# First attention: projections of heads 0-3 in the first half of a batch, heads 4-7 at its end, and TensorE's other work in small pieces

## The chip, the cores and the metric

The kernel runs on one core of a Trainium2 chip. Its time is the device time of one execution in microseconds. Five engines work side by side, each on its own list of instructions and in its order: PE (TensorE, matrix products), DVE (VectorE), ACT (ScalarE), POOL (GpSimd) and SP, which here only issues transfers. They meet at semaphores: an instruction adds to a count, another engine waits until the count has reached a value. Transfers (DMA) are issued by SP, ACT and POOL and run on 16 shared DMA engines.

## The reference

The network has two layers, each of an attention and a feed-forward part, on x of 16 batches, 128 rows (D) and 256 positions (T). What the change touches is the first attention, for each of the 16 batches:

```python
dk = D // NH                              # NH = 8 heads of 16
q = xt @ Wq.T                             # xt: x transposed, (T, D)
qh = q.reshape(B, T, NH, dk).transpose(0, 2, 1, 3)
scores = scale * einsum('bhqd,bhkd->bhqk', qh, qh)
logits = (scores * cmask + (1.0 - cmask) * NEG) * rmask
attn = softmax(logits, axis=-1)
ctx = einsum('bhqk,bhkd->bhqd', attn, qh)
out = ctx @ Wo.T
```

Queries, keys and values are one and the same projection. The mask is 0 or 1 for each position of a batch. Behind it come a gated feed-forward part whose weights are looked up in a table of 16 values, a second attention with 16 heads, and a mixture of four experts.

## The kernel before, in words

**Stages.** The first attention runs over the 16 batches as a software pipeline, with buffers of two batches (`par` is 0 or 1). While batch i has its scores computed for the row maxima, batch i-1 has its transposed scores, exponentials and contexts, batch i-2 is normalised and multiplied by Wo, and batch i+1 is projected. Beside this, one slice of the feed-forward weights per batch is looked up: ACT fetches one-hot rows (1 MB, `load_hot`, L549), DVE compares them (`one_hot`), PE multiplies 32 small matrices (`look_up`), ACT copies the product out (`looked_up`).

**The data of a batch.** The eight heads are four pairs; a projection (`project`, L759) makes the stacked rows of one pair, 256 columns of PSUM bank PA. Half 0 of PA is pairs 0 and 1 (heads 0-3), half 1 is pairs 2 and 3. For each half ACT writes two bf16 copies, `ks` with a constant row for the maximum and `qs` (`stacks`, L516). DVE subtracts `qs` from PA to get the low parts (`lows`, L1166). SP then patches the tiles by DMA (`patch`, L310): one transfer writes the mask's row into `ks` once `ks` is there, two write the low rows into `qs` and `ks` once `low` is there. The counts `pt0` and `pt1` tell that half 0 and half 1 have landed.

**Scores.** For c = 0..3 and s = 0, 1, `scores` writes half s of PB from the qs and ks columns of one pair, and DVE takes the row maxima of it (`maxima`, L1172). Scores with c = 0, 1 wait for `pt0`, with c = 2, 3 for `pt1`. After the eight, DVE casts the maxima, PE turns them into rows (`max_rows`), and DVE adds them to `qs` (`add_max`, counted by `q2`). Only then may `scores_T` of that batch go; each fills half s of PC, from which ACT takes exponentials (`exps`, L531). `scores_T` waits for the exponential two groups back, `scores` for the maximum two groups back. `contexts` needs all eight exponentials.

**Order of the work.** Each engine's order is written by hand in its `body`, and every wait stalls all that stands behind it on that engine. PE: c = 0: scores, scores_T for both s, then project_v (the values); c = 1: the same, then look_up; c = 2: the same, outputs0 (Wo, of batch i-2), projections 0 and 1; c = 3: the same, projections 2 and 3; then contexts, max_rows, contexts. The outputs share a PSUM bank with the look-up, so outputs0 waits until `looked_up` has read it (count `w0`). SP in `load_next` loads x and a mask and then issues patch 0 and patch 1 of the next batch, in this order. POOL masks x for a later batch once all projections of one are done, and splits contexts into parts.

**Ends.** Batches 0 and 1 are projected ahead of the loop by other code, which stays as it is; the body of the last batch has no projections (`after=False`).

Of the kernel before, what the change touches and what calls it, by code (L numbers as in the profile page):

```python
# [15 lines left out]
B, D, T = 16, 128, 256  # L16
# [23 lines left out]
LPC = 512 // (2 * LG)  # L40
# [38 lines left out]
def program(nc, x, cond, condT, consts, wqT, woT, lut, idx_all, w_emb, b_emb, g_norm, w_qkv, g_q, g_k,  # L79
            w_out, w_outT, w_r, b_r, w_all, out, tok_x, tok_r, idx_low, absent_d):  # L80
    with ExitStack() as ctx:
# [420 lines left out]
        def _(act):  # L502
# [13 lines left out]
            def stacks(b, par, h):  # L516
                o = slice(h * 512, (h + 1) * 512)
                act.wait_ge(S["pq"], 2 * b + h + 1)
                if not (isinstance(b, int) and b < 2):
                    act.wait_ge(S["st"], 8 * (b - 1))  # L520
                nc.scalar.activation(ks[:, par, o], PA[:, o], ACT.Identity, bias=cst[:, C_EV:C_EV + 1]).then_inc(S["ka"], 1)
                nc.scalar.copy(qs[:, par, o], PA[:, o]).then_inc(S["qa"], 1)

# [7 lines left out]
            def exps(b, c):  # L531
                unless_first(act, S["ctx"], b)
                for s in range(2):
                    act.wait_ge(S["st"], 8 * b + 2 * c + s + 1)
                    o = slice(s * 512, (s + 1) * 512)
                    nc.scalar.activation(probs[:, c, o], PC[:, o], ACT.Exp, scale=SCALE0).then_inc(S["ex"], 1)  # L536
# [6 lines left out]
            def looked_up(c):  # L543

                act.wait_ge(S["lmm"], c + 1)
                nc.scalar.copy(w0t[:, :, bass.ds(c * LCOLS, LCOLS)], PD[:, 512:1024].rearrange("p (h c) -> p h c", h=2)
                               ).then_inc(S["w0"], 1)
# [9 lines left out]
            def body(i, par, before=True, after=True):  # L557
                exps(i - 1, 0)
                values(i - 1, 1 - par)
                exps(i - 1, 1)  # L560
                looked_up(i - 1)
                load_hot(i + 1, 1 - par)
                exps(i - 1, 2)
                if before:
                    context_out(i - 2)
                exps(i - 1, 3)
                if after:
                    stacks(i + 1, 1 - par, 0)
                    stacks(i + 1, 1 - par, 1)

            body(1, 1, before=False)
# [179 lines left out]
        def _(pe):  # L751
# [16 lines left out]
            def project_v(b, par, half):  # L768
                pe.wait_ge(S[f"xs{par}"], 16 * (half + 1))
                unless_first(pe, S["cq"], b)  # L770
                for kt in range(KT):
                    ins = mm(PD[:, kt * P:(kt + 1) * P], xs[:, par, kt * P:(kt + 1) * P], wq1[:], start=True, stop=True)
                ins.then_inc(S["v"], 1)
# [32 lines left out]
                if s == 1:  # L806
                    ins.then_inc(S["ctx"], 1)

            def look_up(c, par):
                pe.wait_ge(S["onehot"], c + 1)  # L810
                pe.wait_ge(S["q2"], min(c + 1, B) if isinstance(c, int) else c + 1)
                if isinstance(c, int) and c >= B:
                    pe.wait_ge(S["c"], LAST)
                bank = PD[:, 512:1024].rearrange("p (h c) -> p h c", h=2)
                for j in range(LPC):
                    ins = mm(bank[:, :, j * LG:(j + 1) * LG], hot[:, par, j * P:(j + 1) * P],
                             lutw[:].rearrange("p h g -> p (h g)"), start=True, stop=True)
                ins.then_inc(S["lmm"], 1)

            def max_rows(b):  # L820
                pe.wait_ge(S["mc"], 3 * b + 3)
# [9 lines left out]
            def outputs0(b):  # L831
                pe.wait_ge(S["ct"], b + 1)
                pe.wait_ge(S["w0"], LCH if isinstance(b, int) and b == LAST else b + 2)
                for qt in range(KT):
                    ins = mm(PD[:, 512 + qt * P:512 + (qt + 1) * P], cT[:, qt * P:(qt + 1) * P], wo1[:], start=True, stop=True)
                ins.then_inc(S["wo"], 1)
# [11 lines left out]
            def body(i, par, half, before=True, after=True):  # L848
                for c in range(4):
                    for s in range(2):  # L850
                        scores(i, par, c, s)
                        scores_T(i - 1, 1 - par, c, s)
                    if c == 0:
                        project_v(i - 1, 1 - par, half)
                    if c == 1:
                        look_up(i - 1, 1 - par)
                    if c == 2 and before:
                        outputs0(i - 2)
                    if c >= 2 and after:
                        project(i + 1, 1 - par, 2 * c - 4)  # L860
                        project(i + 1, 1 - par, 2 * c - 3)
                contexts(i - 1, 1 - par, 0)
                max_rows(i)
                contexts(i - 1, 1 - par, 1)
# [267 lines left out]
        def _(dve):  # L1132
# [36 lines left out]
                o = slice(h * 512, (h + 1) * 512)  # L1169
                v.tensor_tensor(low[:, o], PA[:, o], qs[:, par, o], ALU.subtract).then_inc(S["lo"], 1)  # L1170

            def maxima(b, before=False):  # L1172
                for c in range(4):
                    for s in range(2):
                        dve.wait_ge(S["sa"], 8 * b + 2 * c + s + 1)
                        if c == s == 0:
                            unless_first(dve, S["mc"], 3 * b)
                        v.tensor_reduce(nmax[:, c, s, :], PB[:, s * 512:(s + 1) * 512].rearrange("p (a k) -> p a k", k=T),  # L1178
                                        AX.X, ALU.max, negate=True).then_inc(S["max"], 1)
                        if before and 2 * c + s < 3:  # L1180
                            normalise(b - 2, 2 * c + s + 1)
                dve.wait_ge(S["max"], 8 * b + 8)
                unless_first(dve, S["mt"], b)
                cols = mcol.rearrange("p q r (s m) -> p r s q m", s=2)
                v.tensor_copy(cols[:, :, :, :, ROW_MAX], nmax[:]).then_inc(S["mc"], 1)
                dve.wait_ge(S["mc"], 3 * b + 1)
                v.tensor_tensor(cols[:, :, :, :, ROW_MAX_LOW], nmax[:], cols[:, :, :, :, ROW_MAX], ALU.subtract).then_inc(S["mc"], 1)

                v.tensor_copy(mcol[:, :, :, ROW_ABSENT::64].rearrange("p q r s -> p q (r s)"),
                              nbig[:, :, bass.ds(b, 1)].broadcast_to([P, KT, 2 * PAIRS])).then_inc(S["mc"], 1)  # L1190

            def add_max(b, par):
                dve.wait_ge(S["mt"], b + 1)
                v.tensor_tensor(qs[:, par, :], PD[:, 512:1024].bitcast(BF16), qs[:, par, :], ALU.add).then_inc(S["q2"], 1)
# [20 lines left out]
            def body(i, par, half, before=True, after=True):  # L1215
                if before:
                    normalise(i - 2, 0)
                maxima(i, before)
                if after:
                    lows(i + 1, 1 - par, 0)  # L1220
                one_hot(i, par, half)
                add_max(i, par)
                if after:
                    lows(i + 1, 1 - par, 1)

            dve.wait_ge(S["kprep"], 1)
            lows(0, 0, 0)
# [406 lines left out]
```

## Time and profile before

| | us |
|---|---|
| median of 3 runs | 780.7 (778.14 to 783.45) |
| profiled execution | 782.84 |
| its span, first to last instruction | 781.2 |
| PE busy | 605.0 (77%) |
| DVE busy | 430.9 (55%) |
| ACT busy | 322.0 (41%) |
| POOL busy | 111.8 (14%) |
| TensorE's granted clock, mean | 0.863 of 2.4 GHz |

Busy times are sums over the span, so stages of different character are mixed. The first attention lies between about 20 and 298 us. The page cuts the span into 40 slices of 19.5 us; slices 2 to 15 hold that stage. In the rows, `small` is the one tensor that holds xs, qs, ks, low and others, `arena` holds the looked-up weights and the one-hot rows, and `wst` scratch. L764 is a projection, L772 project_v, L780 scores, L792 scores_T, L804 contexts, L816 look_up, L828 max_rows, L835 outputs0; L521 and L522 are stacks, L536 exps, L546 looked_up, L550 load_hot's issue; L1178 maxima, L1170 lows, L1164 one_hot, L1194 add_max; L317 is the issue of the two low-part transfers.

### The profile page before, as it was taken

How to read it: one execution, taken by the hardware profiler on the slowest of the kernel's cores; microseconds unless marked ns; L12 is line 12 of the kernel's file. 1: busy time of each engine (PE TensorE's matmuls, PEld its weight loads, DVE VectorE, ACT ScalarE, POOL GpSimd, SP SyncE). 2: the span in 40 equal slices, each digit the busy share in tenths (PEclk: the TensorE clock that was granted, in tenths of full speed). 3: DMA queues.
4: the chain of work that ended last, by engine and by line, in shares of the span. 5: the costliest groups of instructions: out<-in, count | busy, mean ns of one | idle time of the engine just before them, and what ended most of it. 6: DMA issues, size and time to landing. Idle time of an engine off the chain costs nothing. (4 is left out here: it accounts for less than half of the span.)

```text
span 781.2 us, 15202 instructions
## 1 busy us (share of the span) xinstructions
PE 605.0 (77%) x4891; PEld 375.2 (48%) x4923; DVE 430.9 (55%) x957; ACT 322.0 (41%) x575; POOL 111.8 (14%) x145
## 2 busy tenths in 40 slices
PE   1456788867778869999956787788628999999992
PEld 1134455544455445555533454454414666666662
DVE  2455665675665664334336999999852333333331
ACT  1133454544454543233336777777502222222220
POOL 3401111111111001000000000000011333333321
PEclk9576666786666798999989999999958999999997
DMA  8863333333333320000036566555210111111110
GB/s 281 180 166 79 75 88 96 93 93 76 75 90 87 87 73 2 1 1 0 0 76 179 126 147 146 145 147 137 75 21 28 42 41 40 38 40 43 44 34 3
DMA packets 32739, 62.42 MB, mean 80 GB/s; under 512 B 7109, under 2 KB 19975, under 8 KB 30280
## 3 DMA queue, kind: packets, MB, share of 16 engines
q1 hardware_dynamic: 22112, 23.99, 10.7%
q0 software_dynamic: 6432, 18.46, 10.5%
q10 hardware_dynamic: 4168, 19.61, 9.7%
q8 instruction: 17, 0.28, 0.2%
q14 instruction: 10, 0.08, 0.0%
HBM read 58.81 MB, written 7.82 MB: 85 GB/s over the span
## 5 line engine op out<-in xcount | busy, mean ns | idle before, releaser
L1178 DVE TENSOR_REDUCE nmax<-PB 128x2 f32<-128x512 f32 x128 | 83.7, 677 | 93.8 <-PE PB L780 93.8
L536 ACT ACTIVATE probs<-PC 128x512 f32<-128x512 f32 x128 | 69.5, 595 | 132.2 <-PE PC L792 132.1
L780 PE MATMUL PB<-small 64*128 64x256 bf16 x256 | 46.6, 377 | 69.2 <-DMA small<-small 69.2
L1562 DVE TENSOR_TENSOR probs<-PC,probs 128x1024 bf16<-128x1024 f32 x19 | 23.3, 1225 | 79.9 <-ACT probs L729 65.6
L729 ACT CAST probs<-PC 128x1024 bf16<-128x1024 f32 x19 | 19.2, 1012 | 113.7 <-PE PC L1090 95.6
L764 PE MATMUL PA<-small,wq 128*128 128x256 f32 x128 | 50.6, 534 | 13.9 <-DVE identb L1142 13.9
L1082 PE MATMUL PA<-arena,probs 128*128 x227 | 54.2, 390 | 7.7 <-issue 3.9
L780 PEld LDWEIGHTS PB<-small 64*128 64x128 bf16 x256 | 12.8, 104 | 92.0 <-issue 70.6
L1101 PE MATMUL PD<-arena,probs 128*128 x456 | 53.0, 273 | 2.5 <-issue 2.5
L1082 PE MATMUL PB<-arena,probs 128*128 x210 | 48.6, 379 | 0.9
L1101 PEld LDWEIGHTS PD<-arena,probs 128*128 128x128 bf16 x456 | 44.3, 98 | 8.3 <-issue 3.2
L792 PE MATMUL PC<-small 64*128 64x256 bf16 x256 | 46.4, 376 | 0.9 <-ACT probs L536 0.8
L455 POOL DMA_DIRECT2D arena<-in_w_all x16 | 8.5, 531 | 236.9 <-DVE arena L1416 138.0
L764 PEld LDWEIGHTS PA<-small,wq 128*128 128x128 f32 x128 | 31.1, 270 | 22.8 <-issue 19.0
L661 ACT ACTIVATE probs<-PA,gb 128x1024 f32<-128x1024 f32 x32 | 35.6, 1112 | 15.7 <-PE PA L995 15.7
L1082 PEld LDWEIGHTS PA<-arena,probs 128*128 128x128 bf16 x228 | 22.8, 100 | 35.1 <-issue 15.2
L393 POOL TENSOR_TENSOR arena<-wst,wz 128x256 f32 (+1 forms) x16 | 10.0, 625 | 201.2 <-ACT wst L541 201.2
L804 PE MATMUL PD<-probs,vu 128*32 128x256 f32 x512 | 35.1, 395 | 2.4 <-ACT probs L536 1.4
L1285 DVE TENSOR_TENSOR wst<-PB,wst 128x512 f32<-128x512 f32 (+1 forms) x24 | 16.6, 691 | 36.5 <-PE PB L920 28.2
L477 POOL DMA_INDIRECT out<-probs,tokn x19 | 19.3, 1016 | 116.8 <-DVE probs L1569 116.8
L920 PE MATMUL PB<-arena 128*128 (+1 forms) x143 | 35.8, 386 | 0.1
L920 PE MATMUL PA<-arena 128*128 (+1 forms) x133 | 33.9, 386 | 1.0 <-issue 0.6
(188 smaller groups left out, 1175.5 us busy)
## 6 DMA issues: line engine op xcount, KB each, us to landing
arena<-idx_low ACTq DMA_DIRECT2D x15, 1024.0 KB
wst<-in_w_all SPq DMA_DIRECT2D x48, 256.0 KB, 2.8
arena<-in_w_all POOLq DMA_DIRECT2D x16, 384.0 KB, 6.3
arena<-in_idx_all ACTq DMA_DIRECT2D x1, 2176.0 KB, 11.4
arena<-in_cond SPq DMA_DIRECT2D x16, 128.0 KB, 3.3
small<-in_x SPq DMA_DIRECT2D x16, 128.0 KB, 2.1
small<-small SPq DMA_DIRECT2D x64, 32.0 KB
arena<-idx_low POOLq DMA_DIRECT2D x2, 1024.0 KB, 15.2
```

Source lines behind the costliest of these rows:

```text
L477: pool.indirect_dma_start(out, bass.IndirectOffsetOnAxis(ap=tokn[:, j:j + 1], axis=0), yo[:, j % 2, :], None, bounds_check=TOK - 1, oob_is ...
L536: nc.scalar.activation(probs[:, c, o], PC[:, o], ACT.Exp, scale=SCALE0).then_inc(S["ex"], 1)
L661: nc.scalar.activation(probs[:, 2 * par + c, :], PA[:], ACT.Exp, scale=DK1 ** -0.5, bias=gb[:]).then_inc(S["e3"], 1)
L764: ins = mm(PA[:, pr * T:(pr + 1) * T], wq3[:, pr].rearrange("p a b c -> p (a b c)"), xm[:, par, :], start=True, stop=True)
L780: ins = mm(PB[:, s * 512 + qt * T:s * 512 + (qt + 1) * T], qs[r, par, c * T + qt * P:c * T + (qt + 1) * P], ks[r, par, c * T:(c + 1) * T], ...
L792: ins = mm(PC[:, s * 512 + n * T:s * 512 + (n + 1) * T], ks[r, par, pr * T + kt * P:pr * T + (kt + 1) * P], qs[r, par, pr * T:(pr + 1) * T ...
L804: ins = mm(PD[pr * HS:(pr + 1) * HS, s * T:(s + 1) * T], vu[:, par, kt, 2 * pr + s, :], probs[:, (pr // 2) * KT + kt, o:o + T], start=(kt ...
L920: ins = mm(o, w0(w, which, kt, m), v[:, kt, tok], start=(k == 0), stop=(k == 3 * KT - 1))
L1082: ins = mm(bank[:, n * 512:(n + 1) * 512], v[:, par, xo], w[:, o], start=(k == 0), stop=(k == 3 * KT - 1))
L1101: ins = mm(PD[:, 512:512 + T], v[:, f * P:(f + 1) * P], w[:, o], start=(k == 0), stop=(k == 3 * FT - 1))
L1178: v.tensor_reduce(nmax[:, c, s, :], PB[:, s * 512:(s + 1) * 512].rearrange("p (a k) -> p a k", k=T), AX.X, ALU.max, negate=True).then_inc( ...
L1562: v.tensor_tensor(hT_lo, PC[:], hT_hi, ALU.subtract).then_inc(S["hTl"], 1)
```

## The change

PE's body spreads the projections: 0 and 1 go one each into c = 0 and c = 1, ahead of the second scores of that c; 2 and 3 go into c = 3, one behind each scores_T. The look-up is cut into two halves of 16 products, at the end of c = 1 and in the middle of c = 2; project_v and outputs0 stay where they were in their c. ACT evacuates half 0 right after exps(1), takes looked_up and load_hot behind exps(2), and context_out behind exps(3). Its wait before overwriting a half of ks and qs now counts only the scores_T that read this half. DVE makes the low part of half 0 among the maxima, behind that of (2, 0), and the low part of half 1 between one_hot and add_max.

```diff
@@ ACT, stacks
-                    act.wait_ge(S["st"], 8 * (b - 1))
+                    act.wait_ge(S["st"], 8 * (b - 2) + 4 + 4 * h)
@@ ACT, body
                 exps(i - 1, 1)
+                if after:
+                    stacks(i + 1, 1 - par, 0)
+                exps(i - 1, 2)
                 looked_up(i - 1)
                 load_hot(i + 1, 1 - par)
-                exps(i - 1, 2)
+                exps(i - 1, 3)
                 if before:
                     context_out(i - 2)
-                exps(i - 1, 3)
                 if after:
-                    stacks(i + 1, 1 - par, 0)
                     stacks(i + 1, 1 - par, 1)
@@ PE, look_up: takes part_ (0, 1 or None for all)
-                for j in range(LPC):
+                for j in range(*{None: (0, LPC), 0: (0, LPC // 2), 1: (LPC // 2, LPC)}[part_]):
...
-                ins.then_inc(S["lmm"], 1)
+                if part_ != 0:
+                    ins.then_inc(S["lmm"], 1)
@@ PE, body
                     for s in range(2):
                         scores(i, par, c, s)
                         scores_T(i - 1, 1 - par, c, s)
-                    if c == 0:
-                        project_v(i - 1, 1 - par, half)
-                    if c == 1:
-                        look_up(i - 1, 1 - par)
-                    if c == 2 and before:
-                        outputs0(i - 2)
-                    if c >= 2 and after:
-                        project(i + 1, 1 - par, 2 * c - 4)
-                        project(i + 1, 1 - par, 2 * c - 3)
+                        if after and c in (0, 1) and s == 0:
+                            project(i + 1, 1 - par, c)
+                        if (c, s) == (0, 1):
+                            project_v(i - 1, 1 - par, half)
+                        if (c, s) == (1, 1):
+                            look_up(i - 1, 1 - par, 0)
+                        if (c, s) == (2, 0):
+                            look_up(i - 1, 1 - par, 1)
+                        if (c, s) == (2, 1) and before:
+                            outputs0(i - 2)
+                        if after and c == 3:
+                            project(i + 1, 1 - par, 2 + s)
@@ DVE, maxima: takes low_at
+                        if low_at is not None and (c, s) == (2, 0):
+                            lows(b + 1, low_at, 0)
@@ DVE, body
-                maxima(i, before)
-                if after:
-                    lows(i + 1, 1 - par, 0)
+                maxima(i, before, 1 - par if after else None)
                 one_hot(i, par, half)
-                add_max(i, par)
                 if after:
                     lows(i + 1, 1 - par, 1)
+                add_max(i, par)
```

## Rows read from the trace of the kernel before

**Rows 1.** The page's slices: clock granted to TensorE, in tenths of full speed, 19.5 us each.

```profile
PEclk9576666786666798999989999999958999999997
```

**Rows 2.** Windows: length, busy us of PE, PEld, DVE, ACT, POOL; clock, DMA, GB/s.

```profile
160.50:176.80 16.30, 12.21 (x121) 7.89 (x121) 10.70 (x19) 7.77 (x15) 2.01 (x3) 0.73 0.37 91
```

**Rows 3.** Timeline, PE: first scores of the first and the last full batch.

```profile
43.75 0.71 PE L780 MATMUL PB<-small 64*128 64x256 bf16 x4 [9.30 <-DMA small<-small]
...
277.32 0.81 PE L780 MATMUL PB<-small 64*128 64x256 bf16 x4 [3.19 <-DMA small<-small]
```

**Rows 4.** Waits from 60.4 to 277.3 us: total us, times, longest.

```profile
PE PB L780 <- DMA small<-small: 49.5, 13, 5.8
```

**Rows 5.** Timeline of one batch, 160.5 to 176.8 us: start, us, engine, line.

```profile
164.43 0.78 PE L780 MATMUL PB<-small 64*128 64x256 bf16 x3
...
164.63 0.58 ACT L546 CAST arena<-PD 128x512 f32 x1
...
164.78 0.64 ACTq L550 DMA_DIRECT2D arena<-idx_low  x1
...
165.77 1.22 PE L835 MATMUL PD<-wo,wst 128*128 128x128 f32 x4
...
168.34 0.40 PE L780 MATMUL PB<-small 64*128 64x256 bf16 x4
...
168.76 1.29 DVE L1178 TENSOR_REDUCE nmax<-PB 128x2 f32<-128x512 f32 x2 [2.41 <-PE PB L780]
...
168.89 1.13 PE L764 MATMUL PA<-small,wq 128*128 128x256 f32 x4
...
168.98 1.08 ACT L536 ACTIVATE probs<-PC 128x512 f32<-128x512 f32 x2 [1.58 <-PE PC L792]
...
169.95 0.69 ACT L521 ACTIVATE small<-PA,cst 128x512 bf16<-128x512 f32 x1
...
170.12 1.07 PE L804 MATMUL PD<-probs,vu 128*32 128x256 f32 x16
...
171.25 0.69 DVE L1170 TENSOR_TENSOR small<-PA,small 128x512 bf16<-128x512 f32 x1
...
171.81 1.07 PE L804 MATMUL PD<-probs,vu 128*32 128x256 f32 x16
...
171.85 1.28 DVE L1164 TENSOR_SCALAR arena<-arena,cst 128x4096 bf16<-128x4096 bf16 x1
...
171.96 1.12 SPq L317 DMA_DIRECT2D small<-small  x2
...
173.05 0.68 DVE L1194 TENSOR_TENSOR small<-PD,small 128x1024 bf16<-128x1024 bf16 x1
...
176.80 0.62 PE L780 MATMUL PB<-small 64*128 64x256 bf16 x3 [3.92 <-DMA small<-small]
```

**Rows 6.** Short windows in and behind the same batch: columns as in rows 2.

```profile
162.00:164.00 2.00, 2.00 (x31) 1.26 (x30) 1.60 (x4) 1.03 (x3) 0.00 (x0) 0.50 0.07 23
...
172.00:174.00 2.00, 0.88 (x16) 0.26 (x8) 2.00 (x3) 0.18 (x1) 0.00 (x0) 1.00 0.62 147
...
174.00:177.00 3.00, 0.20 (x2) 0.14 (x3) 0.95 (x2) 0.00 (x0) 0.00 (x0) 0.63 0.24 56
```

**Rows 7.** Timeline, PE: the same operations elsewhere, at the other clock.

```profile
133.93 1.91 PE L764 MATMUL PA<-small,wq 128*128 128x256 f32 x4
...
288.71 0.68 PE L772 MATMUL PD<-wq,small 128*128 128x128 f32 x4 [0.60 <-DVE small L1200]
...
295.42 3.02 PE L804 MATMUL PD<-probs,vu 128*32 128x256 f32 x32
```

**Rows 8.** Timeline of the batch before 127.3 us: DMA issues, and the scores behind them.

```profile
115.75 0.65 ACTq L550 DMA_DIRECT2D arena<-idx_low  x1
...
123.49 1.50 SPq L317 DMA_DIRECT2D small<-small  x2
...
127.28 0.62 PE L780 MATMUL PB<-small 64*128 64x256 bf16 x3 [2.96 <-DMA small<-small]
```

More of the change, by code:

```diff
@@ L807, in contexts, with look_up @@
                     ins.then_inc(S["ctx"], 1)
[L809 to L813, printed above, removed]
+            def look_up(c, par, part_=None):
+                if part_ != 1:
+                    pe.wait_ge(S["onehot"], c + 1)
+                    pe.wait_ge(S["q2"], min(c + 1, B) if isinstance(c, int) else c + 1)
+                    if isinstance(c, int) and c >= B:
+                        pe.wait_ge(S["c"], LAST)
                 bank = PD[:, 512:1024].rearrange("p (h c) -> p h c", h=2)
-                for j in range(LPC):
+                for j in range(*{None: (0, LPC), 0: (0, LPC // 2), 1: (LPC // 2, LPC)}[part_]):
                     ins = mm(bank[:, :, j * LG:(j + 1) * LG], hot[:, par, j * P:(j + 1) * P],
                              lutw[:].rearrange("p h g -> p (h g)"), start=True, stop=True)
-                ins.then_inc(S["lmm"], 1)
+                if part_ != 0:
+                    ins.then_inc(S["lmm"], 1)
             def max_rows(b):
@@ L1170, in lows, with maxima @@
                 v.tensor_tensor(low[:, o], PA[:, o], qs[:, par, o], ALU.subtract).then_inc(S["lo"], 1)
-            def maxima(b, before=False):
+            def maxima(b, before=False, low_at=None):
                 for c in range(4):
```

## The prediction

> **What bounds the kernel now.** The slices of the page [rows 1] locate the change: it touches only the first attention, slices 2 to 15, where no engine is full and TensorE's granted clock averages 0.7. A window laid over one batch [rows 2] has PE busy for 12.2 of 16.3 us, DVE for 10.7 and ACT for 7.8: a latency loop, not a full engine. The starts of the first and the last of the 15 full batches [rows 3] are 233.6 us apart, so 14 intervals of 16.68. The table of waits [rows 4] names the loop: in 13 batches PE sat 49.5 us, 3.8 each, until the patch DMAs of heads 0-3 had landed. The timeline of one batch [rows 5] shows why: PE projects the last pair at 168.89, ACT evacuates from 169.95, when its last exponentials are out, the low part follows at 171.25, its two DMAs are issued from 171.96 to 173.08, and the scores that need them start at 176.80. PE's other work is done by 172.9.
>
> The clock rides on that gap [rows 6]: granted 1.00 (2.4 GHz) while PE does the last contexts, on average 0.63 over the idle 3 us, in which it falls, and 0.50 (1.2 GHz) two microseconds into the batch, with PE busy throughout. Against a mean of 0.73 in this batch [rows 2] that makes over half of its time at 1.2 GHz, behind one gap.
>
> **The change, part by part.** No working instruction is added or removed; orders and waits change. I walk one new batch. Zero is the end of add_max, when scores_T may go; prices are start to start. At 2.4 GHz: two score groups of one (c, s) 0.4 together, one projection 0.56 (a pair is 1.13, x4 matmuls), contexts 1.07 a half, transposes 0.62 (what is left between the halves, 170.12 to 171.81) [rows 5], project_v and outputs0, four like matmuls each, 0.7 [rows 7]. For half a look-up I take 0.5 at either clock, an estimate: all 32 small matmuls end where the scores of 164.43 start, and the span of a c leaves them 1 us. ACT: 0.54 an exponential (1.08 for two), 1.1 for ks and qs (0.69 the first, a like one overlapping it), 0.58 look-up copy. DVE: 0.65 a maximum (1.29 for two), casts 1.1 (170.05 to 171.25), one_hot 1.2, lows and add_max 0.6 each, all start to start [rows 5]. I add about 0.15 for each hand-over between engines, as from the last matmul to the reduction behind it in rows 5.
>
> *Projections 0 and 1 move ahead* (c = 0 and 1, first half). They need xm, made a batch earlier, and the lows of the batch before: both long done. c = 0: 0.2 + 0.56 + 0.4 + 0.7 = 1.85. c = 1: two groups of 0.4, projection 0.56, half a look-up 0.5: 1.85. The scores wait for maxima two groups back; the first ends at 1.3, behind DVE's transpose, and PE wants its bank at 1.95: 0.
>
> *ACT: stacks of half 0 ahead of exps(2), looked_up behind it.* The looser wait (4 of the 8 st counts of batch b - 2) is satisfied there. But outputs0 on PE waits for looked_up, and now sits right behind scores_T(2,1) while ACT still owes the second exps(1) (ends 4.0), stacks 1.1, exps(2) 1.1, the copy 0.6: 6.85 with hand-over. PE is through at 5.1 and idles 1.9 us; behind it are queued scores(3), projections 2 and 3. Today outputs0 starts at 165.77 and the copy at 164.63, so nothing waits [rows 5]. c = 2 costs 7.7 - 3.8 = 3.9, exactly today's leg (164.43 to 168.33), which is full of work.
>
> *Lows of half 0 inside the maxima*, 0.6: DVE waits for qs until 5.25 and does the low by 5.9, under PE's new idle time: 0 on the path. If outputs0 did not wait, this would be next: max(2,1) would come 1 us late.
>
> *c = 3*: two groups and two projections, 1.9, and the last exponential: 2.15, contexts from 9.85; today 1.8.
>
> *Tail*: PE has contexts, transposes, contexts: 2.8, free at 12.55. DVE: maxima end at 9.6, casts 1.1, one_hot 1.2, lows(1) 0.6 (its qs is there at 11.2), add_max 0.6: 13.15. The low of half 1 now stands in front of add_max, 0.6 on the path, and scores_T waits for it at 13.2. The tail is 3.45 instead of 2.8 plus the 3.9 gap.
>
> *Queues.* SP's program is unchanged: x and mask loads, then patch 0, patch 1; only its waits end earlier. Patch 0 is issued from 5.9 to 7.1 and needed at 12.55. The landing was 3.7 us after the last issue ended in rows 5 (173.08 to 176.80) and 2.3 in another batch (124.99 to 127.28) [rows 8]: 9.4 to 10.8, hidden with 1.7 to spare. Patch 1 is issued from 12.6 to 13.75 and is needed only by scores(2,0), 3.8 into the next batch, at 17.0; 2.3 to 3.7 later is 16.1 to 17.4, so 0 to 0.4 late; I take 0, since the likeliest batch comes out over 1 us longer than this walk, all of it before c = 2 of the next batch is wanted. POOL's product waits for all projections of a batch, which end where they did, and has over a batch of slack: 0. context_out goes behind exps(3), under the contexts, 0.4 before max_rows asks for it: 0. The split look-up issues the same 32 matmuls: 0.
>
> Sum at 2.4 GHz throughout: 1.85 + 1.85 + 3.9 + 2.15 + 3.45 = **13.2 us**. The same walk at 1.2 GHz (projection 0.95, four in 1.91; outputs0 and project_v 1.22; contexts 1.5, 32 in 3.02; transposes 1.0, an estimate from the ratio of the others; groups 0.25 each, an estimate too [rows 5, 7]) is 2.9 + 2.45 + 4.35 + 2.9 + 4.3 = **17.0 us**, slightly worse than now, for today's tail runs at 2.4 GHz. So the clock decides, and these are the ends of that unknown. The idle time left in a batch is one stretch of 1.9 us behind short look-ups and one of about 0.7. Rows 6 show a fall in a gap of 3.9; by 168.89 the projections run at the high price. I expect falls in some batches, ending sooner because six long pieces are spread over the batch: a third of the time at 1.2 GHz, 13.2 + 3.8/3 = **14.5 us**. That third is a judgement, between none and all.
>
> The section on HAM oscillation of "TensorE: Matmul & The Clock Gate" in the Trainium skill says that a wait for data in every round of a loop throttles the array each time; by that rule alone the sum would be the 13.2. The same page's section on psum-queue depth-cycling says that frequent micro-idles between groups make the clock oscillate too, which speaks against this change: many small waits could keep the toll. By it the sum goes towards 17.0.
>
> Fourteen intervals save (16.68 - 14.5) x 14 = 30.5 us. The last batch, without projections, also takes the new order: outputs0 there waits for an exponential, the copy and the hand-overs, 1.3 more. Net 29.2. The profiled execution took 782.8 us (span 781.2 and 1.6 around it), the runs' median is 780.7, 2.1 less: **751.5 us**.
>
> **Rivals.**
> *Full clock (0.12).* The gap gone, the clock stays up: 13.2, saving 48.7 - 1.3 = 47.4: 733. For it: the clock stayed at 1.00 in 2 us of which PE was busy for 0.88 [rows 6]. Against: the 1.9 us behind outputs0.
>
> *Patch 1 becomes the wait (0.18).* The 1 MB of one-hot rows is issued by ACT 0.15 us after the look-up copy starts, and the patch landed 12.0 us after that issue in rows 5 (164.78 to 176.80) and 11.5 in rows 8 (115.75 to 127.28), steadier than the 3.7 and 2.3 from its own. So patches may end with that transfer. The rows would be issued at 6.4, patch 1 land at 18.4, 1.4 late at scores(2,0); this second gap, next to the outputs0 one, costs the clock: about 0.9 more. Period 15.5, saving 16.5 - 1.3: 765.5.
>
> *Low clock throughout (0.06).* 17.0: 4.5 + 1.3 more, 786.5, within 1%: the change would not do what it says.
>
> *Patch 0 gets caught (0.06), the slower side.* Its DMAs start moving at about 8, just as the one-hot rows do. If its packets are held until those end, it lands at 6.4 + 12.0 = 18.4 where scores(0,0) could start at 12.55, and the period is 18.9: 14 x 2.2 + 1.3 = 32 more, 813. It decides from a landing later than about 16, where the removed 3.5 us are used up. Against it: the one-hot rows are issued at 6.4 and patch 0's first two DMAs by 6.5, so most of it is ahead of them.
>
> "DMA: Bandwidth & Descriptors" of the Trainium skill, section on queues, rings and completion order, says an engine takes turns between its queues packet by packet. By it patch 0 is delayed by some packets, not held to the end, and this rival falls away; no trace row here shows it for a patch in mid-transfer.
>
> **How the numbers follow.** My case has 0.58, at 14.0 to 15.0 us a batch: 744.5 to 758.5. The range takes in the full clock and the late patch 1: 731 to 768, leaving out the two bad cases and the tails. About 1% (8 us) is what can be told from no change. Faster by over 1%: 0.58 + 0.12 + 0.18 = 0.88; within: 0.06; slower: 0.06.
>
> **What would show it.** Intervals between batch starts of 14 to 15 us; PE's wait for the patch DMA at the first scores near zero; a new idle stretch of 1.3 to 2 us on PE before outputs0, released by ACT's look-up copy; granted clock near 0.83 in the stage; the low of half 0 between two maxima; the rest of the trace, from 300 us on, shifted only. Wrong if PE still waits for DMA in every batch (which half tells which rival), if the clock stays near 0.5 or 0.7, or if outputs0 does not wait.

## The result, and the profile after

The changed kernel took 805.8 us (median of 4 runs, 800.7 to 807.3), the kernel before 780.2: a ratio of 1.031 with a 95% interval of 1.025 to 1.037. Forecast were 751.5. The profiled execution took 804.5 us with a span of 802.8. Times below are medians of all runs of a kernel; the ratios and their intervals leave out its runs in a slower state, which matters most in experiment 4.

The first up-projection behind the stage starts at 317.5 us where it started at 298.6: 18.9 of the 21.6 us of span lie in the first attention. The page's slices of the changed kernel, whose clock row answers to [rows 1], show PE busier and its clock higher, and yet more time:

```profile
PE   1489888888779868999985878787636999999993
...
PEclk9997978858986776999997899999967999999997
```

Two windows over single batches, columns as in [rows 2]. Of the 13 batches from 61.3 to 290.0 us, eleven took 16.2 to 18.0 us, like the first, and two took 21.0 and 19.6, like the second.

```profile
130.00:146.90 16.90, 13.34 (x120) 7.23 (x120) 10.80 (x19) 7.92 (x15) 2.84 (x3) 0.90 0.33 86
...
163.60:184.60 21.00, 19.75 (x120) 10.06 (x121) 10.18 (x18) 8.01 (x15) 2.83 (x3) 0.52 0.25 68
```

In the first the clock did what I had hoped, 0.90 against 0.73 (it was 0.89 or more in eight of the 13), and the batch is still 16.9 us. From 69.4 to 297.6 us, outputs0 to outputs0, 13 intervals average 17.55 against 16.68. The table of waits of the changed kernel, from 60 to 300 us (total, times, longest; compare [rows 4]), names two of PE's waits:

```profile
PE PB L781 <- DMA small<-small: 21.3, 10, 3.9
...
PE PD L838 <- ACT arena L546: 17.6, 14, 1.3
```

The second is the wait at outputs0 that was predicted. The first should not be there: it is the wait that the change was to remove. The timeline of one batch (start, us, engine, line) answers to [rows 5]:

```profile
130.02 0.39 PE L781 MATMUL PB<-small 64*128 64x256 bf16 x2 [2.39 <-DMA small<-small]
...
136.49 0.64 ACTq L550 DMA_DIRECT2D arena<-idx_low  x1
...
136.67 1.44 SPq L317 DMA_DIRECT2D small<-small  x2
...
137.46 0.68 PE L838 MATMUL PD<-wo,wst 128*128 128x128 f32 x4 [1.25 <-ACT arena L546]
...
138.07 0.39 PE L781 MATMUL PB<-small 64*128 64x256 bf16 x2
...
138.30 0.38 PE L793 MATMUL PC<-small 64*128 64x256 bf16 x2
...
138.61 0.70 PE L765 MATMUL PA<-small,wq 128*128 128x256 f32 x2
...
146.91 0.39 PE L781 MATMUL PB<-small 64*128 64x256 bf16 x2 [2.30 <-DMA small<-small]
```

First: patch 0 is issued from 136.67 to 138.11. That starts 6.7 us into the batch, where it was 11.5 before (171.96 in the batch from 160.49), and still the scores wait for it until 146.91. It did not take 2.3 to 3.7 us to land but 8.8. In front of it, at 136.49, ACT issued the 1 MB of one-hot rows; from there to the scores it is 10.4 us. In the nine batches from 78.8 us on whose first scores wait, it is 9.7 to 11.5 and mostly 10.2 to 10.9. (The tenth wait of the table, 0.5 us at 66.43, is one for patch 1.) Second: one group of scores and scores_T, 138.07 to 138.61, takes 0.54 us. In [rows 5] both groups of a c stood in 168.34 to 168.89, 0.55. Both figures run from the first matmul to the start of the next piece. At 1.2 GHz it is 0.96 for one (below) against 0.98 for both (162.49 to 163.47 in the kernel before):

```profile
176.33 0.60 PE L781 MATMUL PB<-small 64*128 64x256 bf16 x2
...
176.73 0.63 PE L793 MATMUL PC<-small 64*128 64x256 bf16 x2
...
177.29 1.22 PE L765 MATMUL PA<-small,wq 128*128 128x256 f32 x2
```

The groups s = 0 and s = 1 use partitions 0 to 63 and 64 to 127. Side by side they run almost in the time of one; with a projection between them each takes the full time, so a broken pair costs 1.08 in place of 0.55, and 1.92 in place of 0.98. The two theories to test are thus the held patch and the broken pairs.

### The profile page after: what moved, and what is told of

It is laid out like the page before. It is cut to its first block and busy times, and to the rows that moved or that the text cites. A ratio compares the mean times of both kernels' runs of the same rounds, so it can differ in the third digit from the quotient of the medians.

```text
span 802.8 us, 15202 instructions
## 1 busy us (share of the span) xinstructions
PE 644.3 (80%) x4891; PEld 379.0 (47%) x4923; DVE 434.5 (54%) x957; ACT 325.1 (40%) x575; POOL 124.8 (16%) x145
## 3 DMA queue, kind: packets, MB, share of 16 engines
q1 hardware_dynamic: 22112, 23.99, 10.4%
## 5 line engine op out<-in xcount | busy, mean ns | idle before, releaser
L536 ACT ACTIVATE probs<-PC 128x512 f32<-128x512 f32 x128 | 75.1, 599 | 151.9 <-PE PC L793 150.9
L1184 DVE TENSOR_REDUCE nmax<-PB 128x2 f32<-128x512 f32 x128 | 87.5, 688 | 87.6 <-PE PB L781 86.0
L781 PE MATMUL PB<-small 64*128 64x256 bf16 x256 | 55.4, 319 | 37.2 <-DMA small<-small 37.2
L765 PE MATMUL PA<-small,wq 128*128 128x256 f32 x128 | 60.3, 568 | 14.0 <-DVE identb L1148 14.0
L793 PE MATMUL PC<-small 64*128 64x256 bf16 x256 | 56.6, 323 | 0.8 <-ACT probs L536 0.8
L1107 PE MATMUL PD<-arena,probs 128*128 x456 | 54.7, 278 | 2.5 <-issue 2.5
L393 POOL TENSOR_TENSOR arena<-wst,wz 128x256 f32 (+1 forms) x16 | 21.4, 1336 | 221.0 <-ACT wst L541 221.0
L805 PE MATMUL PD<-probs,vu 128*32 128x256 f32 x512 | 51.3, 542 | 1.4 <-ACT probs L536 1.3
L765 PEld LDWEIGHTS PA<-small,wq 128*128 128x128 f32 x128 | 26.0, 250 | 32.2 <-issue 31.6
L974 PE MATMUL PB<-wqkv,small 128*128 128x512 f32 x64 | 34.0, 657 | 2.1 <-ACT small L633 2.1
```

Source lines behind the costliest of these rows:

```text
L765: ins = mm(PA[:, pr * T:(pr + 1) * T], wq3[:, pr].rearrange("p a b c -> p (a b c)"), xm[:, par, :], start=True, stop=True)
L781: ins = mm(PB[:, s * 512 + qt * T:s * 512 + (qt + 1) * T], qs[r, par, c * T + qt * P:c * T + (qt + 1) * P], ks[r, par, c * T:(c + 1) * T], ...
L793: ins = mm(PC[:, s * 512 + n * T:s * 512 + (n + 1) * T], ks[r, par, pr * T + kt * P:pr * T + (kt + 1) * P], qs[r, par, pr * T:(pr + 1) * T ...
L805: ins = mm(PD[pr * HS:(pr + 1) * HS, s * T:(s + 1) * T], vu[:, par, kt, 2 * pr + s, :], probs[:, (pr // 2) * KT + kt, o:o + T], start=(kt ...
L974: ins = mm(PB[:, 0:512], xnT[:, kt, :], wqkv[:, kt, 0:512], start=(kt == 0), stop=(kt == KT - 1))
L1107: ins = mm(PD[:, 512:512 + T], v[:, f * P:(f + 1) * P], w[:, o], start=(k == 0), stop=(k == 3 * FT - 1))
```

## The experiments

"Before" was run beside each set of experiments and took 781.6, 781.9 and 782.6 us.

**1. Pairs side by side again.** All of PE's other pieces stand behind both s of their c, and the look-up is whole again at c = 1.

```diff
-                        if after and c in (0, 1) and s == 0:
-                            project(i + 1, 1 - par, c)
...
+                    if after and c in (0, 1):
+                        project(i + 1, 1 - par, c)
+                    if c == 0:
+                        project_v(i - 1, 1 - par, half)
+                    if c == 1:
+                        look_up(i - 1, 1 - par)
...
```

> The changed kernel with PE's pieces moved out from between the two score groups of a c (s = 0 and s = 1 stand side by side again; look-up whole again at c = 1); ACT's and DVE's orders as changed. Theory A (the broken pairs are the loss: in the trace of the changed kernel a group of scores and scores_T takes 0.53 us at 2.4 GHz and 0.96 at 1.2, where both groups together took 0.55 and 1.04 before): four pairs get 0.26 to 0.45 us back each, 1.1 to 1.8 a batch, and scores start sooner in every c, so 14 batches give 15 to 30 us, to 775 to 790; the time of the scores in the trace falls by nearly half. Theory B (the patch of heads 0-3 is held behind the one-hot rows and sets the period: 10.4 us from the issue of the rows to the first scores): only what comes between the first scores and the issue of the rows (6.5 us now) gets shorter, by about 0.8; the period goes from 16.9 to 16.1 in undisturbed batches, and PE's wait at the first scores grows from 2.3 to 3.5: 785 to 795.

Measured 798.4 us, ratio 1.019 (1.013 to 1.025). Only 7 us came back, and PE's wait for the patch (same view as above) more than doubled:

```profile
PE PB L781 <- DMA small<-small: 47.3, 14, 4.9
```

From the issue of the rows to the first scores it was 10.8 to 11.6 us in all 14 batches. The time saved by pairs went into the wait: what theory B said, at the slow end of its range.

**2. The changed kernel with 32 KB of rows.** The looked-up weights are left stale, so the output is wrong; all instructions stay.

```diff
-                act.dma_start(hot[:, par, :], hot_rows(c)).then_inc(...)
+                act.dma_start(hot[:, par, 0:P], hot_rows(c)[:, :, 0:P]).then_inc(...)
```

> The changed kernel, but from batch 2 on only 128 of the 4096 columns of one-hot rows are fetched (32 KB in place of 1 MB); all instructions stay, and the looked-up weights are left stale. Theory B (the patch of heads 0-3 waits behind these rows): PE's wait for the patch at the first scores, 26 us in the stage, is gone, and the time falls by 20 to 35 us, to 770 to 785, since the clock also falls less often. Theory A (broken pairs alone are the loss, the patch takes its 2.3 to 3.7 us whatever else moves): the waits stay and the time stays within 4 us of 805.

Measured 780.3 us, ratio 0.996 (0.992 to 0.999): 25 us less than the changed kernel. From 60 us on no wait for the patch is left in the table.

The changed kernel's own trace has the matching case, with all of the rows. In the long batch from 163.59, patch 0 was issued 0.75 us ahead of the rows:

```profile
173.49 1.12 SPq L317 DMA_DIRECT2D small<-small  x2
...
174.24 0.64 ACTq L550 DMA_DIRECT2D arena<-idx_low  x1
```

The DMA view counts the packets of SP's queue (q1) and of ACT's (q10). From 173.49 to 176.00:

```profile
q10 hardware_dynamic: 8, 0.07, 15.0%
q1 hardware_dynamic: 102, 0.07, 8.3%
```

All 102 packets of the patch (34 of them under 512 B) have gone, and its last landing signal is at 175.82, 1.2 us behind the end of its issue. In the batch from 130.02, where the rows were issued 0.2 ahead of it, 54 of the 102 had gone from 136.67 to 139.50; from 139.50 to 141.90 only rows moved, and the last signal came at 146.79:

```profile
q10 hardware_dynamic: 27, 0.22, 32.3%
q1 hardware_dynamic: 54, 0.03, 3.8%
...
q10 hardware_dynamic: 39, 0.32, 53.9%
```

So about half of a patch passes beside the rows and the other half waits. The two batches of this trace with the patch 0.75 us ahead (at 173.49 and 244.20) had it in after 1.2 us; 0.06 ahead (68.17) was not enough.

**3. Both.**

> Both edits: pairs of score groups side by side, and only 32 KB of one-hot rows a batch (looked-up weights left stale). This is the schedule that the prediction walked through, with its wait at outputs0. If both causes together are the whole failure: period 13.5 to 14.5 us, 735 to 755. If another cause is left (the wait at outputs0 or the low part ahead of add_max costing more than 1.9 and 0.6 us, or the clock staying low): 760 or more.

Measured 731.9 us, ratio 0.939 (0.932 to 0.945), a little better than expected. This is the order of events that the prediction had walked through, and 13 intervals from outputs0 at 63.91 to outputs0 at 227.05 average 12.55 us. A pair in this kernel, eight matmuls side by side:

```profile
161.69 0.40 PE L781 MATMUL PB<-small 64*128 64x256 bf16 x4
...
161.92 0.39 PE L793 MATMUL PC<-small 64*128 64x256 bf16 x4
...
164.04 0.68 PE L838 MATMUL PD<-wo,wst 128*128 128x128 f32 x4 [1.73 <-ACT arena L546]
```

The pair's last matmul ends at 162.31, 0.62 from its start, as in [rows 5]. The wait at outputs0 is 1.73, near the 1.9 of the walk. The two edits give 7 and 25 us alone and 74 together: each fault hides the other, since the held patch sets the period as long as it is there, and broken pairs fill the time otherwise. Of the 48 us between experiments 2 and 3, 3.2 for each of 15 batches, 1.63 show in one batch of each at full clock:

```profile
138.43:151.51 13.08, 11.77 (x125) 6.84 (x121) 10.24 (x19) 7.82 (x15) 1.95 (x2) 1.00 0.11 28
...
132.74:144.19 11.45, 9.62 (x125) 6.17 (x121) 9.58 (x18) 7.76 (x15) 1.97 (x2) 1.00 0.14 36
```

The rest is the clock: other batches of experiment 2 took 17.2 us at 0.70, the slower ones of experiment 3 12.9 to 13.4.

**4. The kernel before with broken pairs.** Projection 2, look_up, outputs0 and project_v each stand between the groups of their c:

```diff
-                    if c == 0:
+                        if c == 0 and s == 0:
                             project_v(i - 1, 1 - par, half)
...
```

> The kernel before, with one thing changed: in each c one of PE's other pieces (project_v, look_up, outputs0, projection 2) stands between the groups s = 0 and s = 1 in place of behind both. ACT and DVE untouched. Theory A (two groups side by side run on both halves of the array at once, and the pieces between them undo that): each of four pairs costs 0.26 us at 2.4 GHz and 0.45 at 1.2, 1.0 to 1.8 a batch, in a loop where PE's end sets the patch: 15 batches, 795 to 807. Theory B alone: the loop is set by the patch behind the last projection and pieces between groups only shift work: 778 to 784.

Measured 788.4 us over ten runs from 776.2 to 791.1, ratio 1.004 (0.999 to 1.009): no change that can be told, and between the two expectations. The broken pairs do show in the trace, but they eat into the wait: from 60 to 230 us PE is busy for 144.8 us in place of 131.5 and its scores wait for patches for 15.4 in place of 42.6. Behind a held patch this kernel is the wrong place to weigh pairs.

**5. The rows issued early.** Look-up at c = 0, project_v at c = 1, on top of experiment 1:

```diff
                 exps(i - 1, 0)
+                looked_up(i - 1)
+                load_hot(i + 1, 1 - par)
+                exps(i - 1, 1)
                 values(i - 1, 1 - par)
-                exps(i - 1, 1)
```

> The pairs side by side as in the first experiment, the full 1 MB of one-hot rows, but PE does the look-up already at c = 0 (project_v moves to c = 1) and ACT copies it out and issues the next rows right behind exps(0). If patch 0 is held until the rows are in (10.4 to 11 us from their issue to the first scores), the rows' issue about 2.5 us after the first scores lets it land at 13 to 13.5, about when it is needed: period 13 to 13.8, 735 to 750, PE's wait for DMA at the first scores under 1 us a batch, and no wait at outputs0. If instead any overlap with the 1 MB costs a patch a fixed delay, wherever the rows start, the wait of about 3.4 us stays and the time is 775 to 800.

Measured 760.3 us, ratio 0.972 (0.969 to 0.976). Of the wait at outputs0 0.8 us is left, once from 60 to 300 us, and the kernel is 38 us faster than with the late issue, but the patch still came 2 us late:

```profile
122.76 0.64 ACTq L550 DMA_DIRECT2D arena<-idx_low  x1
...
128.81 1.12 SPq L317 DMA_DIRECT2D small<-small  x2
...
135.65 0.39 PE L781 MATMUL PB<-small 64*128 64x256 bf16 x2 [2.00 <-DMA small<-small]
```

Issue of rows to scores is 12.9 here and 12.2 to 13.3 in all batches, more than the 10.4 to 11 that I had put in. The expectation missed by 10 us on that; that the start of the rows moves the landing, it had right.

**6. The rows issued late**, behind exps(3), on top of experiment 1:

```diff
                 looked_up(i - 1)
-                load_hot(i + 1, 1 - par)
                 exps(i - 1, 3)
+                load_hot(i + 1, 1 - par)
```

> The first experiment's kernel (pairs side by side, 1 MB of rows) with only the issue of the rows moved, from behind looked_up to behind exps(3). Held-patch theory: patch 0 now goes ahead of the rows and PE's wait at the first scores is gone, but patch 1 is issued behind them and is held: the wait moves to the scores of c = 2, and the rows' issue about 6.5 us behind the start of c = 2 plus 10.5 gives a period of about 17: 785 to 805. If the hold were special to patch 0, or came from the amount moved in a batch: no wait at c = 2 and 740 to 755, or the old wait at the first scores and 798.

Measured 797.9 us, ratio 1.022 (1.018 to 1.025). The wait moved:

```profile
138.98 0.64 ACTq L550 DMA_DIRECT2D arena<-idx_low  x1
...
142.67 1.11 SPq L317 DMA_DIRECT2D small<-small  x2
...
143.37 0.40 PE L781 MATMUL PB<-small 64*128 64x256 bf16 x3
...
151.22 0.63 PE L781 MATMUL PB<-small 64*128 64x256 bf16 x3 [3.63 <-DMA small<-small]
...
153.97 1.19 PE L838 MATMUL PD<-wo,wst 128*128 128x128 f32 x4 [1.48 <-ACT arena L546]
```

The first scores (143.37) go at once, those of c = 2 (151.22, ahead of outputs0) wait 3.6 us for patch 1, 12.2 behind the rows' issue. Patch 0, now issued 3 us ahead of the rows (135.73 to 136.85), had landed 1.2 us later, at 138.05. Whichever patch is issued behind the rows is held.

**7. The kernel before with 32 KB of rows** (the edit of experiment 2).

> The kernel before, with 32 KB of one-hot rows a batch from batch 2 on in place of 1 MB (looked-up weights left stale). In it patch 0 is issued when the rows have been moving for 7 us. Held-patch theory: it still loses 1 to 1.5 us a batch to them (landing 2.3 to 3.7 us after the last issue in place of about 2): 14 to 20 us less, 762 to 768. If the before kernel's landing was its own and the rows had no part in it: within 3 us of 781. It also bounds what the small rows give by themselves in the other experiments.

Measured 729.2 us, ratio 0.933 (0.927 to 0.938), far below both expectations. The patch's own share of the gap is now seen:

```profile
152.35 1.13 SPq L317 DMA_DIRECT2D small<-small  x2
...
154.79 0.39 PE L780 MATMUL PB<-small 64*128 64x256 bf16 x2 [1.54 <-DMA small<-small]
```

1.31 us from the end of the issue to the scores, in nearly every batch the same, in place of 2.3 to 4.0; and with the gap down to 1.5 the clock is 0.89 from 60 to 230 us against 0.70, and 1.00 in the batch that ends here. The old order, with the patch as late as it can be, is as fast as the best of the new ones once the rows are small.

**8. The low part of half 1 behind add_max**, on top of experiment 5.

> The kernel with the rows early, with DVE's low part of half 1 put back behind add_max, as in the kernel before. The prediction charged 0.6 us a batch on the path for the low part in front of add_max: 8 us less than the kernel with the rows early if add_max sets the start of the next batch. If patch 0's landing or PE's contexts set it, nothing: within 3 us of it. If patch 1 then comes too late for c = 2, more, up to 8 us.

Measured 762.8 us, ratio 0.975 (0.972 to 0.979), beside 0.972 of experiment 5. The 0.6 us a batch that the prediction charged for it are not to be had here, where the patch's landing still sets the period.

**9 to 11. The rows as four transfers of 256 KB**, 2 KB a partition in place of 8. Two are issued where the one was, the other two one exponential later:

```diff
+                n = LHOT // 4
+                for k in (2 * part_, 2 * part_ + 1):
+                    act.dma_start(hot[:, par, k * n:(k + 1) * n], hot_rows(c, k)).then_inc(...)
...
-                    dve.wait_ge(S[f"hot{par}"], 16 * half)
+                    dve.wait_ge(S[f"hot{par}"], 64 * half)
```

In the kernel before:

> The kernel before, with the same 1 MB of one-hot rows a batch fetched as four transfers of 256 KB (2 KB a partition in place of 8 KB), two behind looked_up and two behind exps(2). If a patch is held because its small packets take turns with 8 KB packets on the same DMA engines (packets of 2 KB would pass four times as fast), PE's wait at the first scores falls from 3.8 us towards the 1.5 us seen with 32 KB of rows: 735 to 760. If the hold is a matter of the bytes in flight, or of the issues' order, the landing stays 12 us behind the first issue of rows, or gets later with the second pair: 780 to 800.

Measured 752.1 us, ratio 0.961 (0.956 to 0.967). PE's wait at the first scores (60 to 300 us):

```profile
PE PB L785 <- DMA small<-small: 22.6, 13, 2.6
```

1.7 us a batch, nearly the 1.5 of 32 KB. The packet records say how: the last packet of the rows ends 8.3 to 9.2 us behind their first issue, where it was 10.1 to 11.0 with one transfer, so that they are nearly in when the patch is issued. In the changed kernel:

> The changed kernel with the rows in four transfers of 256 KB, two behind looked_up and two behind exps(3). Packets taking turns: patch 0 is freed or nearly, the time comes near the 780 us of the same kernel with 32 KB of rows, 778 to 792, and what is left above the kernel before is the broken pairs. Bytes in flight: 800 to 815.

Measured 771.6 us, ratio 0.984 (0.980 to 0.989), lower than expected and lower than with 32 KB by 9 us; the clock from 60 to 230 us was 0.83 against 0.80, and why is open. Patch 0 is still held, for less time: its last signal comes 4.3 to 4.7 us behind the end of its issue. In three batches the third quarter was late enough to show for how long. In the one from 151.87, with the quarters issued at 158.36, 159.16, 163.76 and 164.56 and the patch at 158.53, the patch landed at 164.48, and until then ACT's queue had moved

```profile
q10 hardware_dynamic: 272, 0.52, 28.9%
```

the 256 packets of the first two quarters with 8 closing ones each, and nothing of the third, whose first packet came at 165.18. In the changed kernel with its pairs side by side:

> The changed kernel with the pairs of score groups side by side and the rows in four transfers of 256 KB. Packets taking turns: both faults mended, near the 732 us of the same kernel with 32 KB of rows: 732 to 755. Bytes in flight: 790 to 805, as with the single transfer (798).

Measured 733.3 us, ratio 0.936 (0.932 to 0.941). It computes everything, and it beats both kernels, by 48 and 72 us. In its table of waits no wait for the patch is left; the longest of PE's is the one at outputs0, 1.6 a batch:

```profile
PE PD L843 <- ACT arena L548: 24.5, 15, 1.7
```

**12. Broken pairs in the kernel before, with 32 KB of rows.**

> The kernel before with 32 KB of rows a batch (729 us) and one piece of PE's other work between the two groups of each c, as in the fourth experiment (looked-up weights stale). With the wait behind the rows out of the way the broken pairs should show in full: at 2.4 GHz 0.26 us for each of four pairs and 15 batches is 16 us, at 1.2 GHz 0.45 is 27, and the later scores and maxima add to it: 745 to 770. If broken pairs cost nothing and the 48 us between the changed kernel's two forms with 32 KB of rows came from something else in its order: 726 to 734.

Measured 752.3 us, ratio 0.961 (0.954 to 0.968): 23 us over experiment 7 (22 by the ratios), 1.5 a batch. Two batches at full clock are 13.58 us (144.77 to 158.35) against 11.94 (142.85 to 154.79). The 1.64 between them are not four broken pairs alone, which would be four times 0.53, or 2.1. One pair forms anew across two c, s = 1 of c = 0 with s = 0 of c = 1:

```profile
146.08 0.40 PE L780 MATMUL PB<-small 64*128 64x256 bf16 x4
...
149.38 0.68 PE L835 MATMUL PD<-wo,wst 128*128 128x128 f32 x4 [0.59 <-ACT arena L546]
```

and 0.59 is a new wait at outputs0, which now comes ahead of ACT's copy. In experiment 7 the pair of c = 1 was not side by side either (144.26 and 144.82).

The medians side by side:

| rows per batch | kernel before | with broken pairs | changed | changed, pairs whole |
|---|---|---|---|---|
| 1 MB, one transfer | 781.6 | 788.4 | 805.8 | 798.4 |
| 1 MB, four transfers | 752.1 | not run | 771.6 | 733.3 |
| 32 KB | 729.2 | 752.3 | 780.3 | 731.9 |

And the clock over a fixed stretch of the stage, 60 to 230 us (columns as in [rows 2]), in this order: before, changed, changed with 32 KB of rows, experiment 11.

```profile
60.00:230.00 170.00, 131.51 (x1212) 82.47 (x1212) 107.36 (x194) 78.70 (x152) 20.19 (x30) 0.70 0.35 85
```
```profile
60.00:230.00 170.00, 142.91 (x1180) 76.84 (x1176) 105.76 (x189) 78.30 (x148) 25.78 (x28) 0.81 0.33 84
```
```profile
60.00:230.00 170.00, 156.02 (x1296) 85.33 (x1292) 114.82 (x207) 86.24 (x165) 29.65 (x31) 0.80 0.10 28
```
```profile
60.00:230.00 170.00, 142.30 (x1587) 89.42 (x1585) 134.81 (x255) 102.88 (x200) 29.34 (x38) 0.89 0.36 112
```

The counts of matmuls (x1212, x1180, x1296, x1587) say how much work got done in the same 170 us. The third row has PE busy for 92% of the time, and its waits are those at outputs0 (13.8 us): there the pieces themselves, at the clock they get, are the bound.

## Why the prediction was wrong

**The step that failed first is "Queues", the landing of patch 0.** It took the landing from its own issue (2.3 to 3.7 us), put patch 0 at 9.4 to 10.8 us of the batch and called it hidden. It landed at 16.9 (130.02 to 146.91). The time from the issue of the rows had been read: the change moves patch 0 from 7 us behind that issue [rows 5] to 0.2 behind it (136.49 and 136.67), so that nearly all of the rows are still to come. Experiments 2 and 6 show cause and place, experiment 7 that the kernel before was already bound by it.

**The rival "patch 0 gets caught" is what happened**, at a chance of 0.06. Its mechanism was right: the packets of patch 0 start as the rows do and come in with their end. Its price was too high: 12.0 us from the rows' issue against 10.4 measured, a period of 18.9 against 16.9. I had argued it away by who is issued first: patch 0 from 5.9 us of the batch, the rows at 6.4. As a rule that holds (1.2 us to the landing where the patch was 0.75 ahead), but the order was misjudged by less than a microsecond. The rows were issued at 6.5, as walked, and the patch at 6.7: ACT's stacks of half 0 began at 134.67, 4.65 into the batch against 4.0, behind two legs of PE that took 4.5 us against 3.7, and the issue of the rows went out 0.24 ahead of the look-up copy (136.49 and 136.73) and not behind its start.

I had also weighed the section on queues, rings and completion order of "DMA: Bandwidth & Descriptors" in the Trainium skill, where an engine takes turns between queues packet by packet, and concluded that this frees patch 0. The conclusion was wrong. I had put the delay at "some packets"; what the section says is that an engine drains a whole packet, typically 9 to 17 descriptors (the single pieces of a transfer), before it switches. The transfer of the rows has 128 packets in the profile and closes with 8 small ones, each of the patch's two low-part transfers with 16. If that means 8 engines against 16, each of the 8 has 16 of the 128, which can be one packet in the section's sense; taking turns and being held are then the same for the half of the patch that shares these engines. Experiment 10 fits this, with the patch in behind exactly two quarters. No run tests it, and none shows that the size of a packet matters by itself: with 2 KB ones the patch waited for 256 of them, with 8 KB ones for 128.

**The price of a score group failed second.** For scores and scores_T of one (c, s) the walk took 0.4 us at 2.4 GHz and 0.5 at 1.2, so 0.8 and 1.0 for a c. [Rows 5] show 0.55 for a c at 2.4 GHz: the price was too high for a pair side by side and too low for a broken one, 1.08 and 1.92. The sentence "c = 0: 0.2 + 0.56 + 0.4 + 0.7" even put the projection between the groups. The four legs to the contexts were 2.35, 2.2, 3.5 and 3.1 us in the changed kernel (130.02, 132.37, 134.56, 138.07, 141.14) against 1.85, 1.85, 3.9 and 2.15. The expectations of experiments 1, 4 and 12 price a broken pair at 0.26 to 0.45 us, which is the excess of one group; a pair has two, so it is 0.53 at 2.4 GHz and 0.94 at 1.2, or 2.1 and 3.8 a batch if all four were whole before. Measured between experiments 2 and 3 are 1.63 a batch at full clock, where the pair of c = 1 is not side by side in experiment 3 either (134.37 and 134.93) and the wait at outputs0 is 0.5 shorter in experiment 2, and 3.2 on average, with a clock of 0.80 against 0.90 from 60 to 230 us.

**Right were** the wait at outputs0 (1.25 in the changed kernel, where late pieces ate some of it, and 1.73 where they did not; predicted 1.9); the low part of half 0 among the maxima, which delayed nothing that could be seen; and, by luck, the clock: 0.81 over 60 to 230 us with 0.83 expected, but out of batches at 0.90, 0.71 and 0.52. With both faults away (experiment 3) the walk had the order and the wait right and its sum too high. The rival of the full clock (13.2, 733) meets the measured 731.9 by luck: the batch at 1.00 took 11.45 us, not 13.2, and the mean was 12.55 at 0.90. **Priced too high** were the four legs, 9.75 against 8.89 (132.74 to 141.63), and the tail, 3.45 against 2.56 (to 144.19), with the low part of half 1 ahead of add_max in it: in that trace PE waited for add_max four times from 60 to 300 us, 1.6 us in all. Small slips that decide nothing: the casts take 1.2 us in [rows 5], not 1.1, and the legs at 1.2 GHz add up to 16.9, not 17.0.

The first rival, patch 1 as the next wait, had the mechanism too, 12 us from the rows' issue. It came out where the rows were issued late (experiment 6) and once, for 0.5 us, in the changed kernel. And the slower end of the clock's range, 17.0 us for a batch at 1.2 GHz, was too good for broken pairs: the batch from 163.6 took 21.0 at 0.52, and four c at 1.92 in place of 1.0 are 3.7 us of it.

**Open:** why the rest of a patch comes in when it does. The last packet of the rows ends 10.1 to 11.5 us behind their issue in the changed kernel, in the kernel before and in experiment 5 alike. The first scores follow within 0.2 us of it where the patch was issued 0.2 behind the rows (eight of the nine waits; the other was 1.1 before it), 1.0 to 1.8 later in the kernel before (7 to 8 behind) and 1.4 to 2.3 later in experiment 5 (4 to 7 behind). So the end of the rows sets the hold in all of them, and the different totals come from that last stretch, which no run explains. Also open is what sets the clock where PE hardly waits (0.80 in experiment 2, 0.83 in experiment 10).

## What to carry to other kernels

A transfer's landing time read from a trace belongs to what else was in flight; before moving a small transfer, look for the large one beside it and place or cut that one first (here four pieces in place of one, two of them issued an exponential later, gave 30 us to the kernel before). Do not put other matrix work between two matmul groups that use different halves of the rows: price them as a pair, and a lone group at the full price of the pair. When two waits hide each other, an experiment that removes one shows little; run both together before calling either harmless.

## What the runs showed of the hardware

PE's two groups on partitions 0 to 63 and 64 to 127 took 0.55 us together and one alone 0.54 at 2.4 GHz, 0.98 and 0.96 at 1.2.

A patch issued 0.2 to 1.0 us behind 1 MB in 8 KB pieces was waited for until 8.4 to 9.9 us after the end of its issue (changed kernel, experiment 1), and 1.3 us after it with 32 KB in flight (experiment 7). Issued 0.75 us ahead of the 1 MB it landed after 1.2.

A wait of 1.5 us in every batch left the clock at 1.00 in the batch from 142.85 of experiment 7, while in experiment 2, with 1.25 us at outputs0 as its only wait, the batch from 168.97 ran at 0.70. The waits alone do not give the clock.

POOL's first product of context_parts took 0.61 us before and 1.47 in the changed kernel (medians of 15 and 13), where the later context_out puts it beside DVE's one_hot, here from 140.86 to 142.15; nothing waited for it:

```profile
140.86 1.29 DVE L1170 TENSOR_SCALAR arena<-arena,cst 128x4096 bf16<-128x4096 bf16 x1
...
141.15 1.47 POOL L393 TENSOR_TENSOR arena<-wst,wz 128x256 f32 x1 [13.87 <-ACT wst L541]
```
